# Two key projections and two value groups of each batch in other PSUM banks

## The reference

```
x = x + layernorm(attention(layernorm(x)))
x = x + layernorm(ffn(layernorm(x)))

# attention (Nystrom, 16 heads of 16 channels, 64 landmarks = means of 16 tokens)
Q, K, V   = x @ w_qkv
kernel1   = softmax(Q  . K_l)      # 1024 x 64
kernel2   = softmax(Q_l . K_l)     # 64 x 64
kernel3   = softmax(Q_l . K)       # 64 x 1024
out       = (kernel1 @ inverse(kernel2, 6 steps)) @ (kernel3 @ V) @ w_proj

# ffn: 8 experts; each reconstructs x, the one with the least loss adapts the output
idx = argmin over e of mean((relu(x @ Wd1[e] + bd1[e]) @ Wd2[e] + bd2[e] - x)^2)
out = x @ W_base + b_base + relu(x @ Wa_down[idx] + ba_down[idx]) @ Wa_up[idx] + ba_up[idx]
```

## Time and profile before

| | us |
|---|---|
| median of 3 runs | 2115.79 |
| lowest and highest | 2112.59, 2116.33 |
| the profiled execution | 2112.14 |
| its span, first to last instruction | 2110.4 |
| mean granted clock of TensorE in it | 0.989 |

### The profile page before, as it was taken

How to read it: one execution, slowest core, us unless ns; L and a number is a source line. 1 busy time by engine, 2 the same in 40 slices (tenths; PEclk the granted TensorE clock), 3 DMA queues, 4 the chain that set the end, 5 groups by cost and what they waited for, 6 DMA issues and landing times.

```text
span 2110.4 us, 59639 instructions
## 1 busy us (share of the span) xinstructions
PE 1956.5 (93%) x25418; PEld 1266.6 (60%) x25418; DVE 1453.7 (69%) x3333; ACT 864.5 (41%) x1515; POOL 689.1 (33%) x904
## 2 busy tenths in 40 slices
PE   4889999999999999999999999999999999999966
PEld 2655747566574755657566574756657475565734
DVE  4668676776758677675866867677676767767562
ACT  3435344343434434344443534434343444434332
POOL 4243152433325233242522315243232523324030
PEclk9989999999999999999999999999999999999989
DMA  7213152331524223151331415123151422314020
GB/s 169 55 51 82 32 129 45 84 70 22 141 32 118 56 73 71 32 142 32 98 65 53 101 32 132 41 84 69 24 139 32 121 53 76 68 32 121 13 61 20
DMA packets 233578, 151.29 MB, mean 72 GB/s; under 512 B 153097, under 2 KB 204337, under 8 KB 233298
## 3 DMA queue, kind: packets, MB, share of 16 engines
q1 hardware_dynamic: 233314, 147.49, 30.0%
HBM read 37.52 MB, written 16.78 MB: 26 GB/s over the span
## 4 chain that ended last, share of the span: by engine, by line
PE 59%; POOL 11%; DVE 10%; SPq 8%; issue 5%; ACT 4%; DMA 2%; POOLq 0%; ACTq 0%; DVEq 0%
PE NS L1048 13%; PE ringF L1258 11%; SPq L445 6%; PE ringA L1217 5%; PE ringF L1291 4%; PE ringF L1243 3%; POOL QS L577 3%; DVE stats L1459 3%; PE ringA L1115 3%; POOL yout L577 3%; PE KV L1129 3%; SPq L415 2%; PE KV L1187 2%; PE ringA L1091 2%; POOL rstd L541 2%
## 5 line engine op out<-in xcount | busy, mean ns | idle before, releaser
L1258 PE MATMUL ringF<-x,H 128*128 128x256 f16 x1536 | 237.9, 273 | 0.0
L1650 DVE TENSOR_REDUCE mx<-ringA 128x8 f32<-128x512 f32 x256 | 174.9, 684 | 61.1 <-PE ringA L1091 61.0
L729 ACT ACTIVATE E<-ringA,score_scale 128x512 f32<-128x512 f32 x256 | 174.5, 688 | 98.5 <-PE ringA L1115 98.4
L1258 PE MATMUL ringF<-H 128*128 128x128 f16 x1024 | 204.4, 220 | 1.4 <-DVE H L1735 1.4
L1701 DVE SCALAR_TENSOR_TENSOR X<-X,NS 128x320 f32<-128x320 f32 x160 | 78.1, 488 | 167.1 <-PE NS L1048 161.9
L942 PE MATMUL ringA<-xT,wqkv 128*128 128x512 f16 x768 | 176.9, 380 | 16.5 <-ACT QS L747 11.7
L1243 PE MATMUL ringF<-wd,x2T 128*128 128x512 f16 x768 | 185.7, 380 | 3.1 <-DMA x2T<-x 1.5
L737 ACT ACTIVATE E<-ringA,score_scale 128x512 f32<-128x512 f32 x256 | 158.9, 686 | 66.7 <-PE ringA L1146 66.7
L1636 DVE TENSOR_REDUCE mx<-ringA 128x1 f32<-128x512 f32 x256 | 160.3, 684 | 28.9 <-PE ringA L1082 28.8
L538 POOL TENSOR_SCALAR vtmp<-mv,eps_ffn 128x8 f32<-128x8 f32 x15 | 4.8, 318 | 522.8 <-DVE mv L1470 522.8
L538 POOL TENSOR_SCALAR vtmp<-mv,eps_ln 128x8 f32<-128x8 f32 x31 | 9.7, 312 | 497.1 <-DVE mv L1470 497.1
(11 more groups left out here) (284 smaller groups left out, 4177.9 us busy)
## 6 DMA issues: line engine op xcount, KB each, us to landing
KS<-stage SPq DMA_DIRECT2D x384, 64.0 KB, 2.0
QS<-stage SPq DMA_DIRECT2D x384, 64.0 KB, 2.0
xin<-in_L_attn_x_dram SPq DMA_DIRECT2D x16, 1024.0 KB, 11.5
xres<-in_L_attn_x_dram SPq DMA_DIRECT2D x16, 1024.0 KB, 8.0
out_dram<-yout SPq DMA_DIRECT2D x15, 1024.0 KB, 5.5
QS<-LB SPq DMA_DIRECT2D x16, 512.0 KB, 4.4
wup<-in_L_ffn_Wa_up_dram SPq DMA_DIRECT2D x2, 512.0 KB
out_dram<-yout SPq DMA_DIRECT2D x2, 512.0 KB, 2.9
```

What stands on the lines that cost most here:

```text
L729: A(E[:, k % ESLOTS, :], ps[:, :], ACT.Exp, scale=score_scale[:, 0:1]).then_inc(freed["s3"].sem, 1)
L1258: ins = MM(dst, H[:, a, t, own], src, start=first and i == 0, stop=last and i >= 3, skip_group_check=True)
L1650: V_.reduce_max(mx1[:, t, 8 * h:8 * h + 8], take(b, "m1", k)[:, :].rearrange("p (a m) -> p a m", a=8), AX.X)\
```

## The change

`pk` 0 and 1 leave the attention's ring for the two banks of the FFN's ring. At that time the FFN's matmuls of the batch before have not begun, and those of two batches before are read. TensorE waits for that reading (from batch 2 on) ahead of `pk` 0. `pv` 0 goes to `KV`, behind the reader of the last `sv` of the batch before, and `pv` 1 to `NS[1]`, behind the reader of its last `ss`. Since `keep_warm` writes `NS[1]`, TensorE waits for ScalarE's copies of `pv` 0 and 1 ahead of the maxima matmuls, where it waited for the last `ss` before. The ring loses four uses and needs no padding now (87 uses in place of 91 and two of padding): `pk` 2 follows `pl` in its bank, `pk` 3 follows `pr` 2, `kl` follows `pr` 3. No instruction that computes is added, taken out or moved in any engine's order.

```
-        USES_A = ([("pk", k) for k in range(4)] + [("kl", 0), ("ql", 0)] + [("pv", k) for k in range(2)]
+        USES_A = ([("pk", k) for k in (2, 3)] + [("kl", 0), ("ql", 0)]
                   + [("lk", k) for k in range(3)] + [("lq", k) for k in range(2)] + [("pk", k) for k in (4, 5)]
...
             if (kind, k) in USES_A:
                 return ringA[USES_A.index((kind, k)) % 3]
+            if kind == "pv":
+                return (KV, NS[1])[k]
+            if kind == "pk":
+                return ringF[k]
...
-                    ps = get(b, "pk", k)
+                    if k == 0 and b >= 2:
+                        pe.wait_ge(freed["ff"].sem, freed["ff"].at(b - 2, 4))
+                    ps = get(b, "pk", k) if k >= 2 else bank("pk", k)
...
             def values(b, ks):
                 for k in ks:
-                    ps = get(b, "pv", k)
+                    if k < 2 and not first(b):
+                        kind = ("sv", "ss")[k]
+                        pe.wait_ge(freed[kind].sem, freed[kind].at(b - 1, 4))
+                    ps = get(b, "pv", k) if k >= 2 else bank("pv", k)
...
                 kernel2_scores(b)
-                if not first(b):
-                    pe.wait_ge(freed["ss"].sem, freed["ss"].at(b - 1, 4))
+                pe.wait_ge(freed["pv"].sem, freed["pv"].at(b, 2))
                 for k in range(4):
```

## The result

| | us |
|---|---|
| before, median of 19 runs (lowest, highest) | 2112.42 (2107.05, 2121.30) |
| after, median of 19 runs (lowest, highest) | 2120.39 (2117.29, 2125.22) |
| ratio after to before, 95% interval | 1.0035 (1.0025 to 1.0045) |
| span of the profiled execution, before and after | 2110.4, 2115.9 |
| TensorE's mean granted clock, before and after | 0.989, 0.981 |

The changed kernel is 0.35% slower, about 7.4 us of 2112. The two clocks in the table are those of the profiled executions. Over all 19 executions of the changed kernel the mean clock is 0.976 to 0.981, 0.9794 on average; over 29 executions of the kernel before, measured beside the first experiments, it is 0.986 to 0.991, 0.9883 on average. First the page of the changed kernel: the chain that ended last, and the costliest group of the maxima matmuls (out<-in, count, busy, mean ns, idle time before them).

What follows compares the result with a forecast made beforehand. TensorE held 59% of the chain, but VectorE and GpSimd's chain was taken to set the second maxima matmul. 10 x 0.85 less 1 gave +7.5 us on 2115.79, so 2123; the forecast's own range was 2116 to 2133.

Steps and rivals of the forecast that it cites:

- Parts 1 and 2: TensorE's waits before key projection 0 and value group 0 vanish: 0.77 and 0.71 earlier, 1.48 us a batch together.
- Part 3: The new wait for value copies 0 and 1 ahead of the maxima matmuls costs 0.0 us.
- Absorption: Second maxima matmul still waits for VectorE's subtraction for projection 4, so TensorE gains 0 of the 1.48 us a batch.
- the pin: VectorE and GpSimd's chain from attention-output statistics to projection 4's subtraction stands still, holding the second maxima matmul at 545.27.
- The idle stretch: First maxima matmul follows the scores at once; TensorE's idle time before the second grows by 1.48 to 1.6 to 2.0 us.
- SyncE: SyncE's transfers start 0.77 earlier; transposes still need GpSimd's low halves; gain 1 us, range 0.7 to 5.4.
- The clock, how often: Behind the longer idle time TensorE's clock falls in 10 of 15 batches, bounds 0 and 15, for 3.4 us each.
- The clock, what one costs: Slower maxima matmuls and query projections 6 and 7 lose 1.3, less 0.45 covered: 0.85 us a fall, range 0.25 to 1.25.
- A step that I waved away: GpSimd's low halves, needing ScalarE's copy behind projection 7, come late by a little less and don't change a fall's cost.
- The sum: Whole kernel: ten clock falls at 0.85 make 8.5, less 1 from SyncE, +7.5 us; range 0 to +18.
- The rule of the Trainium skill: It warns only of idle gaps between matmul bursts longer than this one; by it TensorE's clock would hold.
- Rival A: Removed waits are absorbed before the second maxima matmul and the clock holds: -1 us, -5 to +1; chance 0.39.

Runs made afterwards that it cites:

- the shorter chain: Two of GpSimd's eight attention-output normalisations moved to ScalarE: on the kernel before 0.9961; on the changed kernel 0.9906, or 0.9916 with six more warming matmuls.
- the run with more warming: Changed kernel with six more warming matmuls a batch, two ahead of the first maxima matmul and four, not one, ahead of the second: 2110.72 us, ratio 0.9993.
- the banks of before and six normalisations: Kernel before with the last two of eight attention-output normalisations moved from GpSimd to ScalarE: 2108.10 us, ratio 0.9961.

## Why the prediction was right, step by step

- **Parts 1 and 2.** Both waits are gone. Key projection 0 starts even while the output projection drains (1155.83 for an end at 1156.00), so the first step is 0.94 and not 0.77. The second is 0.89 and not 0.71 (the scores end at 14.58 in place of 15.47 with the value groups alone), and together the scores end 1.83 earlier where I had 1.48.
- **Part 3.** The new wait ahead of the maxima doesn't appear in the list of waits.
- **Absorption.** The subtraction stayed at 15.5 to 15.8 behind the output projection in all 15 batches. Moving the value groups alone shows the absorption in the time (0.9996), and the shorter chain shows the pin.
- **The idle stretch.** I had the first maxima matmul follow the scores at once. It doesn't: it starts 13.8 to 15.1 behind the output projection, after scores that end at about 13.6, and the list names no releaser. What it waits for by the program is the stack of key projections 0 and 1. Its twelfth transfer was issued 2.1 to 4.1 us earlier, and in all 15 batches it landed 0.09 ahead of the matmul; before, TensorE came at 15.3, behind landings at 14.4 to 15.1, and hardly met this. So a second pin stood close before the first. The idle time is therefore split in two, 1.47 and 0.80 in the batch shown. The growth of the total before the maxima matmuls, 34.2 - 10.4 = 23.8 us, is near the 15 x 1.48 = 22.2 that I had reckoned with. ScalarE's copies of the landmark stacks also hold TensorE a little more (7.8 us in place of 2.7), which I had not seen.
- **SyncE.** Its queue was freed as forecast and gave little. I took 1 us of a range of 0.7 to 5.4. The four batches without a fall are 0.07 shorter than the same four before (1 us over 15 batches) and 0.24 shorter than all of before (3.6 us); four batches can't decide between the two, and the 14 of the run with more warming, at 125.21, show no gain. SyncE's waits for GpSimd grew by 24.4 us, 1.6 a batch and not 0.7: where the clock fell, GpSimd's low halves themselves start 23.65 to 24.44 behind the output projection, in the four other batches at 23.25.
- **The clock, how often.** Eleven falls, forecast ten, of 3.4 us each as forecast. That the count is so close is in good part luck: ten was a choice between 0 and 15 by likeness to four idle stretches of the trace before. The page's 9s also say less than I read in them: a slice with a 9 can hold short stretches at 1.2 GHz, as the second does at 70.54.
- **The clock, what one costs.** Forecast 0.85 in a range of 0.25 to 1.25; measured 1.14 against the four neighbours, 0.91 batch by batch against before. The run with more warming says the same from the other side: 1.0035 less 0.9993 is 8.9 us, 0.8 for each of eleven falls, with intervals that leave 0.45 to 1.15. The way is the forecast's way, the two query projections. This is the ninth batch's part of the chain that ended last (start, us, what):

```profile
1174.31 2.73 PE ringA L946 x6
1177.04 0.22 PE ringA L1091
1177.26 1.31 PE ringA L946 x6
1178.60 0.60 ACT stage L685
1179.22 0.69 DVE stage L1593
1179.91 1.21 DVE mx L1644 x2
```

  VectorE's subtraction for projection 7 starts 22.5 to 23.3 behind the output projection in the starred batches and at 21.6 in the others, 1.4 later on average; 0.1 of this is the chain of VectorE and GpSimd itself, 0.2 to 0.3 later in five of the starred batches in both kernels. From this subtraction to the end of the batch it is 102.99 to 103.00 in nine of the eleven and 103.03 to 103.04 in two of the four others, so the lateness passes whole to the end of the batch. What is saved against it are waits for transfers that the other batches had on top. I had 1.3 less 0.45.
- **A step that I waved away.** I wrote that GpSimd's low halves come late by a little less and don't change it. They do wait for ScalarE's copy behind the late projection 7:

```profile
1180.32 2.13 POOL L623 TENSOR_TENSOR x<-yout,x 128x1024 f16<-128x1024 f32 x1 [0.70 <-ACT x L759]
```

  But TensorE waited for the transposed input once in this trace, 0.4 us, and the chain of the ninth batch doesn't pass through GpSimd behind the fall. So nothing shows that they add to the price.
- **The sum.** Forecast 10 x 0.85 - 1 = +7.5. In the two traces, batch by batch: 11 x 0.91 - 15 x 0.07 = +9.0, and -3.1 in batch 0 and -0.5 behind the last batch, which makes the 5.5 between the spans. The medians differ by 8.0, the ratio says 7.4. (With the averages in its place it is 11 x 1.14 - 15 x 0.24 = +8.9, two larger terms of opposite sign; the sum doesn't tell which split holds.) The forecast time of 2123 stood on the median of three runs, 2115.79; over 19 runs that median is 2112.42, so the time came out lower and the difference as forecast.
- **The rule of the Trainium skill** (TensorE: Matmul & The Clock Gate, section "Why this matters for your kernels"), by which the clock should hold, did not hold here: the clock fell in 11 of 15 batches behind 1.93 to 2.28 of idle time in two parts with two matmuls between them (1.47 and 0.80 in the ninth), none of the parts longer than 2.05. The trace decides.
- **Rival A** was right on everything but the clock; the four batches without a fall and the run with more warming matmuls are that rival.

## What to carry to other kernels

A wait at the head of an engine's list is worth its length only if nothing else holds the engine soon after: look for the next thing that it needs from a chain the edit doesn't touch, and compare the two times before and after. Removed waits collect in front of such a pin as one longer idle stretch, and on TensorE a longer stretch can cost the clock, so the edit can lose time without adding any work. Shorten the pin first; the same edit that cost 0.35% was then worth about 0.5%. And before averages of two groups of batches are compared, compare each batch with itself in the other kernel: here that took the price of a fall from 1.14 to 0.91.

## What the runs showed of the hardware

- Whether the clock falls in a given place differs from batch to batch at the same idle time: four batches of the changed kernel kept it with 1.93 to 1.94 of idle time ahead of the second maxima matmul, where six others lost it with 1.93 to 1.95. One of the four, batch 6, with 0.77 and 1.16:

```profile
794.73 0.38 PE L1091 MATMUL ringA<-KS,QlB 96*128 96x512 f16 x1 [0.77 <-issue]
...
796.49 0.39 PE L1091 MATMUL ringA<-KS,QlB 96*128 96x512 f16 x1 [1.16 <-DVE stage L1593]
```

- The last output projection of batch 0 ends between 147.3 and 157.3 in the nine traces (153.5 before, 150.4 after), though the kernels' work up to there is nearly the same. The clock is at 1.2 GHz there in one to four stretches, at other times in each trace. This alone moves a single execution by several us, so that a difference below half a percent can't be read from one run of this kernel.
- One of GpSimd's normalisations is slow where it meets VectorE's addition of two operands in SBUF. In every batch of the changed kernel the normalisation that starts 0.2 to 0.4 behind the start of VectorE's first addition takes 1.52 us; the one already running when the addition starts takes 0.56 like the rest. The slow one is part of the 5.27 for eight of them, and of the 5.33 before. With the banks of before and six normalisations the last one had begun before that addition in every batch, and none took more than 0.56.
